# Attention scores as 32-row products of two units side by side, with scores and transposes in one bank

## The reference

```
x = x + 0.5 * ffn(layernorm(x))
x = x + attn(layernorm(x))
x = x + 0.5 * ffn(layernorm(x))
```

## Time and profile before

| | us |
|---|---|
| median of 3 runs (lowest, highest) | 1555.97 (1555.27, 1557.31) |
| span of the profiled execution | 1558.5 |
| PE busy | 1341.3 (86%) |
| DVE busy | 924.5 (59%) |
| ACT busy | 645.8 (41%) |
| POOL busy | 246.7 (16%) |
| starts of the first and of the last scores product | 526.59 and 1166.33 |

### The profile page before, as it was taken

How to read it: one execution, slowest core, us unless ns; L and a number is a source line. 1 busy time by engine, 2 the same in 40 slices (tenths; PEclk the granted TensorE clock), 3 DMA queues, 4 the chain that set the end, 5 groups by cost and what they waited for, 6 DMA issues and landing times.

```text
span 1558.5 us, 32504 instructions
## 1 busy us (share of the span) xinstructions
PE 1341.3 (86%) x8323; PEld 858.5 (55%) x8324; DVE 924.5 (59%) x3760; ACT 645.8 (41%) x2323; POOL 246.7 (16%) x279
## 2 busy tenths in 40 slices
PE   4412799999996899989899999989994699999996
PEld 4411466666664456656566565656653366666664
DVE  5789444444443567787687877787784244444442
ACT  1114322232222476656566665656661132222221
POOL 4323001000102101021111112020212101100100
PEclk9999999999998899999999999999996799999998
DMA  9500442000002101020201111020206221000000
GB/s 301 206 28 31 171 151 58 13 13 13 17 13 88 48 21 42 22 56 21 57 9 38 33 32 46 21 56 21 56 9 242 59 58 55 17 13 13 13 17 14
DMA packets 57278, 85.55 MB, mean 55 GB/s; under 512 B 8848, under 2 KB 40848, under 8 KB 57168
## 3 DMA queue, kind: packets, MB, share of 16 engines
q1 hardware_dynamic: 50352, 65.49, 13.7%
q0 software_dynamic: 6816, 18.81, 3.4%
HBM read 45.81 MB, written 27.97 MB: 47 GB/s over the span
## 4 chain that ended last, share of the span: by engine, by line
PE 66%; DVE 12%; issue 6%; ACT 2%; POOL 2%; DMA 1%; SPq 1%; another core or an unknown queue 1%; DVEq 0%; ACTq 0%; POOLq 0%
PE bank L797 24%; PE bank L926 9%; PE bank L749 9%; PE bank L815 9%; PE bank L952 6%; PE bank L886 4%; DVE w_all L1364 3%; DVE w_all L1373 2%; PE bank L912 2%; DVE hb L1210 2%; PE bank L963 2%; ACT sl L629 2%; PE bank L763 1%; PE bank L899 1%; POOL sorted_rows L504 1%
## 5 line engine op out<-in xcount | busy, mean ns | idle before, releaser
L709 ACT ACTIVATE w_all<-w_all 128x128 f32<-128x128 f32 x896 | 349.7, 393 | 223.1 <-DVE w_all L1364 222.0
L797 PE MATMUL bank<-w_all,xt 128*128 x1680 | 391.2, 383 | 11.5 <-DVE xt L1222 3.5
L1364 DVE CUSTOM_DVE_ANT_0 w_all<-bank,w_all 128x128 f32<-128x128 f32 x896 | 207.3, 287 | 133.8 <-PE bank L926 123.5
L797 PEld LDWEIGHTS bank<-w_all,xt 128*128 128x128 f16 x1680 | 165.3, 98 | 196.7 <-issue 37.3
L1210 DVE SCALAR_TENSOR_TENSOR hb<-bank,ew,sl 128x512 f32<-128x512 f32 x140 | 105.1, 751 | 207.2 <-ACT sl L629 207.2
L815 PE MATMUL bank<-w_all,ht 128*128 x1680 | 206.2, 273 | 1.2 <-DVE yt L1235 1.2
L629 ACT ACTIVATE sl<-bank,back 128x512 f32<-128x512 f32 x140 | 95.9, 685 | 238.6 <-PE bank L797 221.8
L749 PEld LDWEIGHTS bank<-ident,w_all 128*128 128x128 f32 x896 | 112.6, 142 | 119.9 <-issue 113.2
L815 PEld LDWEIGHTS bank<-w_all,ht 128*128 128x128 f16 x1680 | 164.2, 98 | 19.4 <-issue 1.7
L709 ACT ACTIVATION_READ_ACCUMULATOR w_all<-w_all 128x1 f32 x896 | 169.8, 189 | 0.0
L1373 DVE COPY w_all<-bank 128x512 f32<-128x512 f32 x224 | 153.7, 686 | 1.3 <-PE bank L749 1.2
(11 more groups left out here) (163 smaller groups left out, 1585.5 us busy)
## 6 DMA issues: line engine op xcount, KB each, us to landing
big<-sorted_rows SPq DMA_DIRECT2D x70, 130.5 KB
saved<-w_all SPq DMA_DIRECT2D x16, 512.0 KB
w_all<-saved SPq DMA_DIRECT2D x4, 2048.0 KB, 14.2
w_all<-mid SPq DMA_DIRECT2D x9, 512.0 KB, 3.6
big<-in_L_attn_hidden_states SPq DMA_DIRECT2D x8, 512.0 KB, 4.2
w_all<-in_L_ffn_gate_w SPq DMA_DIRECT2D x8, 512.0 KB
w_all<-in_L_ffn_up_w SPq DMA_DIRECT2D x8, 512.0 KB
w_all<-in_L_ffn_down_w SPq DMA_DIRECT2D x8, 512.0 KB
```

Source lines behind the costliest of these rows:

```text
L709: a = nc.scalar.activation(prob[:, u % NB, h], sbias[:, u % NB, h], ACT.Exp, bias=nmax[:, u % NB, h:h + 1], scale=-1.0, accum_out=rsum[:, ...
L797: mm = nc.tensor.matmul(bank[2 * e + w][:], xt[:, hx, c, :], flat(gu16[:, bass.ds(g * E + e, 1), w, hw, c, :]), start=(i == 0), stop=(i == ...
L1364: i = nc.vector.tensor_tensor_reduce(out=sbias[:, u % NB, h], in0=bank[u % 2][:, h * W:(h + 1) * W], in1=nbias[:, (u % NQ) * HQ + h], scal ...
```

## The change

1. `scores` handles two units of a window at once, every second step. Each of its four products has only 32 rows as its contraction (2 heads), the 32 rows of quarter q, and 256 columns: two key images (one for each head of the pair), so the zeros are needed only between two neighbouring heads. The order is: chunk 0 of unit q0, chunk 0 of unit q0 + 1, chunk 1 of q0, chunk 1 of q0 + 1. The two units lie in different 32-row groups of the array and go to different banks.
2. A unit has one bank, u % 4, for its scores and then for its transposes. So the scores of units u + 2 and u + 3, issued at even u, wait for `copy_pt(u - 1)`; `turn` has no wait for a bank.
3. The heads of a unit change: quarter q has heads 2q, 2q + 1, 8 + 2q, 9 + 2q. Its four value products go to four different strips of 32 partitions; odd quarters accumulate on even ones. The columns of `Wv` and `bv` (by eight small POOL copies) and the rows of `Wo` (by eight DMAs in place of one) are permuted to fit.
4. `km` is now written by ACT: each key block is copied twice, scaled by a mask of zeros and ones, with a masked bias (two small DVE operations and four that make the mask, once). `kt`, the 16 DMAs per batch, their waits and the two memsets of `km` go. There are two `km`, one for even and one for odd batches.
5. The loads of `Wo` and `bo` move behind the loads of the first two batches of activations. POOL waits for them ahead of its first `accumulate`, PE ahead of the first output projection.

```diff
-        km = big[:, 0:H * S].rearrange("p (h s) -> p h s", h=H)
+        km = [big[:, k * 2 * DC * S:(k + 1) * 2 * DC * S].rearrange("p (c e s) -> p c e s", c=DC, e=2) for k in range(2)]
...
+        def head_at(q, i):
+            return (i // 2) * HC + 2 * q + i % 2
+        def slot_at(q, i):
+            return (q // 2) * HC + 2 * i + q % 2
...
-            sp.dma_start(wo_s, Wo.rearrange("(c p) n -> p c n", p=P)).then_inc(aw_loaded, 16)
-            sp.dma_start(bo_s, bo.partition_broadcast(P)).then_inc(aw_loaded, 16)
+            def load_wo():
+                wo_rows = Wo.rearrange("(c m l e i) n -> c e l i m n", c=2, m=DC, l=2, e=2)
+                for k in range(HC):
+                    sp.dma_start(wo_s[k * HD:(k + 1) * HD], wo_rows[k // 4, (k // 2) % 2, k % 2]).then_inc(wo_loaded, 16)
+                sp.dma_start(bo_s, bo.partition_broadcast(P)).then_inc(wo_loaded, 16)
...
                 if not last:
-                    sp.wait_ge(k_ready, b * DC + 2 * DC)
-                    sp.wait_ge(s_done, b * UNITS + 4 * NQ + OPEN)
-                    mask_keys(b + 1, 0)
                     sp.wait_ge(xa_ready, (prep_use(b + 1) + 1) * TB)
                     load_batch(b + 2)
                     shift_values(b + 1, 1 - par)
-                    sp.wait_ge(s_done, b * UNITS + UNITS + OPEN)
-                    mask_keys(b + 1, 1)
...
             load_batch(1)
+            load_wo()
...
+            for m in range(DC):
+                for c in range(2):
+                    pool.tensor_copy(wv_to[:, :, m, c], wv_from[:, :, c, m]).then_inc(wv_ready, 1)
+                    pool.tensor_copy(bv_to[:, m, c], bv_from[:, c, m]).then_inc(wv_ready, 1)
+            pool.wait_ge(wo_loaded, 16 * WO_LOADS)
...
-            def copy_k(b, m):
+            def copy_k(b, par, m):
                 act.wait_ge(proj_done, b * NPROJ + (m + 1))
-                if m == 0:
-                    act.wait_ge(km_loaded[1], b * (16 * HC) + OPEN)
-                nc.scalar.activation(kt[:, m, :], bank[6 + m][:], ACT.Identity, bias=qkb[:, 1, m:m + 1]).then_inc(k_ready, 1)
+                for e in range(2):
+                    a = nc.scalar.activation(km[par][:, m, e, :], bank[6 + m][:], ACT.Identity, bias=kb[:, e, m:m + 1],
+                                             scale=kmask[:, e:e + 1])
+                a.then_inc(k_ready, 1)
...
-            def scores(b, par, u, early):
-                n, q = divmod(u, NQ)
+            def scores(b, par, u, freed):
+                n, q0 = divmod(u, NQ)
                 if u == 0:
-                    pe.wait_ge(km_loaded[0], (b + 1) * (16 * HC) + OPEN)
+                    pe.wait_ge(k_ready, (b + 1) * DC)
                     pe.wait_ge(q_ready, (b + 1) * DC)
-                if u == 3 * NQ:
-                    pe.wait_ge(km_loaded[1], (b + 1) * (16 * HC) + OPEN)
-                if not early:
-                    pe.wait_ge(sb_ready, b * UNITS + (u - 1))
-                nc.tensor.matmul(bank[u % 2][:].rearrange("p (h k) -> p h k", h=HQ),
-                                 qt[par][:, q * HQ // HC, n * STRIDE:n * STRIDE + W],
-                                 km[:, q * HQ:(q + 1) * HQ, n * STRIDE:n * STRIDE + W],
-                                 start=True, stop=True).then_inc(s_done, 1)
-            def turn(b, u, early):
+                if freed is not None:
+                    pe.wait_ge(pt_ready, freed)
+                win = slice(n * STRIDE, n * STRIDE + W)
+                for c in range(DC):
+                    for q in (q0, q0 + 1):
+                        rows = slice(q * HS, (q + 1) * HS)
+                        mm = nc.tensor.matmul(bank[q][:, c * 2 * W:(c + 1) * 2 * W].rearrange("p (e k) -> p e k", e=2),
+                                              qt[par][rows, c, win], km[par][rows, c, :, win], start=True, stop=True)
+                        if c == DC - 1:
+                            mm.then_inc(s_done, 1)
+            def turn(b, u):
                 pe.wait_ge(p_ready, b * UNITS + (u + 1))
-                if not early:
-                    pe.wait_ge(pt_ready, b * UNITS + (u - 1))
                 for h in range(HQ):
-                    tr = transpose(bank[2 + u % 2][:, h * W:(h + 1) * W], prob[:, u % NB, h])
+                    tr = transpose(bank[u % NQ][:, h * W:(h + 1) * W], prob[:, u % NB, h])
...
-                    m, pair = divmod((q * HQ + h) // 2, HC // 2)
-                    mm = nc.tensor.matmul(bank[4 + (par + n) % 2][HS * pair:HS * (pair + 1), m * W:(m + 1) * W],
-                                          va[par][:, n, q * HQ + h, :], pt_s[:, u % 2, h * W:(h + 1) * W],
-                                          start=(h % 2 == 0), stop=(h % 2 == 1))
+                    m = q // 2
+                    mm = nc.tensor.matmul(bank[4 + (par + n) % 2][HS * h:HS * (h + 1), m * W:(m + 1) * W],
+                                          va[par][:, n, slot_at(q, h), :], pt_s[:, u % 2, h * W:(h + 1) * W],
+                                          start=(q % 2 == 0), stop=(q % 2 == 1))
...
-                    if ahead(b, u, last):
+                    if u % 2 == 0 and ahead(b, u, last):
                         b2, u2 = ahead(b, u, last)
-                        scores(b2, par if u2 > u else 1 - par, u2, False)
-                    turn(b, u, first_ and u < 2)
+                        scores(b2, par if u2 > u else 1 - par, u2, None if first_ and u == 0 else b * UNITS + u)
+                    turn(b, u)
...
-                nc.vector.tensor_copy(pt_s[:, u % 2], bank[2 + u % 2][:]).then_inc(pt_ready, 1)
+                nc.vector.tensor_copy(pt_s[:, u % 2], bank[u % NQ][:]).then_inc(pt_ready, 1)
```

More of the change, by code:

```diff
@@ L58 @@
 NPROJ = 2 * DC + TB
-ATTN_LOADS = 9
+ATTN_LOADS = 7
+WO_LOADS = 9
+APADS = 2
+VPERM = 8
+MASK_STEPS = 4
 SHIFTS = 2
@@ L181, in macaron_kernel @@
         xb = part(TB, D)
-        kt = part(DC, S)
         sbias = part(NB, HQ, W)
@@ L196, in macaron_kernel @@
         qkb = part(3, DC)
+        kmask = part(2)
+        kb = part(2, DC)
+        kbits = part(1)
         inv_count = part(NWIN)
@@ L200, in macaron_kernel @@
         assert NGU * CH >= at[0] and at[0] - DC * D - D >= NGU * CH * (G - 1) // G
+        wv_in = sbias[:, 0].rearrange("p h k -> p (h k)")
+        bv_in = sbias[:, 1, 0:2].rearrange("p h k -> p (h k)")
         ct = sb("ct", [P, 2, DC, W])
@@ L331, in _ @@
         def _(sp):
-            for s in km_loaded:
-                sp.sem_inc(s, OPEN)
             def load_x(r, par):
@@ L410, in load_batch @@
                 sp.dma_start(xb, rows_of(b)).then_inc(xb_loaded, 16)
[L412 to L418, removed]
             def shift_values(b, par):
@@ L551, in _ @@
                 for half in range(2):
-                    pool.wait_ge(*((icount_made, 2 * n + half) if n or half else (apads_made, 3)))
+                    pool.wait_ge(*((icount_made, 2 * n + half) if n or half else (apads_made, APADS)))
                     pool.memset(inv_count[half * STRIDE:(half + 1) * STRIDE, n:n + 1],
@@ L557, in _ @@
             pool.wait_ge(aw_loaded, 16 * ATTN_LOADS)
+            wv_from = wv_in.rearrange("p (d c m l e i) -> p d c m e l i", d=DC, c=2, m=DC, l=2, e=2)
+            wv_to = wv_s.rearrange("p d (m c e l i) -> p d m c e l i", m=DC, c=2, e=2, l=2)
+            bv_from = bv_in.rearrange("p (c m l e i) -> p c m e l i", c=2, m=DC, l=2, e=2)
+            bv_to = bv_s.rearrange("p (m c e l i) -> p m c e l i", m=DC, c=2, e=2, l=2)
+            for m in range(DC):
[3 more added lines that the diff above has]
+            pool.wait_ge(wo_loaded, 16 * WO_LOADS)
             def accumulate(b, par, n):
@@ L731, in _ @@
             copy_xnt(prep_use(0))
-            copy_k(0, 0)
-            copy_k(0, 1)
+            copy_k(0, 0, 0)
+            copy_k(0, 0, 1)
             copy_q(0, 0, 0)
@@ L880, in _ @@
             pe.wait_ge(aw_loaded, 16 * ATTN_LOADS)
[L881 removed]
+            pe.wait_ge(apads_made, APADS)
             def project(m, w):
@@ L890, in project_v @@
             def project_v(b, t, ranked):
+                pe.wait_ge(wv_ready, VPERM)
                 if t in (0, 2):
@@ L1005, in batch @@
                             t = int(s[1])
+                            if t == 0:
+                                pe.wait_ge(wo_loaded, 16 * WO_LOADS)
                             project_out(b - 1, 1 - par, t, (v_ready, b * TB + TB) if t < 2 else None)
@@ L1031, in _ @@
             pe.wait_ge(v_ready, TB)
-            scores(0, 0, 0, True)
-            scores(0, 0, 1, True)
+            scores(0, 0, 0, None)
             two_by_two(pe, batch)
@@ L1337, in _ @@
             dve.wait_ge(y_ready, NS + OPEN)
-            nc.vector.memset(km[:, 0:H // 2], 0.0).then_inc(km_zero, 1)
+            mask = Chain(mask_step, 0)
+            mask(nc.vector.tensor_single_scalar(kbits.bitcast(I32), token_no[:, 0:1], 4, ALU.arith_shift_right))
+            mask(nc.vector.tensor_single_scalar(kbits.bitcast(I32), kbits.bitcast(I32), 1, ALU.bitwise_and))
```

(9 more changed lines are left out.)

19 lines of the change are left out of this document (8 added, 11 removed).

## The result

The kernel after takes 1601.72 us (median of 4 runs, 1592.89 to 1611.11) against 1555.62 (1550.70 to 1557.31) for the one before: ratio 1.03, 95% interval 1.0256 to 1.0344. It is slower, as forecast, but by 46 us where +9 was expected. The profiled execution took 1599.55 us, and its span, from the first to the last instruction, is 1596.6. The 1558.5 given for the kernel before is a span too, so it is compared here with 1596.6.

A forecast was written before the change was run, and what follows sets the result against it. PE bound the attention stage; after the change a PE-DVE loop through the shared bank would. Six batches +6, batch 0 +2, batch 7 +2, start -1 made +9: 1567 to 1568 us profiled, 1565 us median, range 1538 to 1630.

The forecast's parts named there:

- the loop: Attention stage: PE and DVE wait on each other through the shared bank; a clean pair costs 4.37 us, 4.12 before.
- rival A: Scores on PE: the 32-row products don't overlap, so scores take 1.72 us a pair; 1633 us, chance 0.24.
- The 2.5 taken off: End of the sum: the profiled execution, 1567 to 1568 us, is 2.5 above the median, giving 1565 us.
- Scores of a pair: PE in attention: a load of 0.10 us and 0.97 of columns, between 0.86 and 1.08, against 1.72 of columns before.
- Values: PE in attention: a unit's value products stay at 0.57 us.
- rival B: Value products on PE: all four go at once, `values` falling from 0.57 to about 0.25 us; 1540 us, chance 0.18.
- Rival C: DVE in attention: its lag already cost time before, so the loop costs nothing net; 1550 to 1556 us, chance 0.08.
- +1.0: Batch 1: pairs of steps sum to 81.04 us against 80.06, a loss applied to each of six batches, +6.
- Start: Start of the kernel: `Wo` and `bo` leave the front of the first activations, two issues of 0.51 us; -1.0 us.
- Key copies: ACT copies each key block twice, +2 x 0.69 us a batch, costing nothing; 1.4 a batch if its cover went.
- The eight copies on POOL: Start: they end before the v projections, some 10 us after POOL is free; otherwise each late microsecond counts once.

The follow-up runs named there:

- fill3: The kernel after, with the four value products of each even quarter issued four times; 1577.22 us, ratio 1.0129 to the kernel before.
- unpaired: The kernel after with its 32-row products, but scores one unit at a time, each waiting for `copy_pt` two units back; 1655.25 us, ratio 1.0641 to before.
- turn_twice: The kernel after, with each of the four transposes of a unit issued twice; 1590.23 us, ratio 1.0229 to the kernel before.
- four_strips: The kernel before, 128-row scores one unit at a time, with heads regrouped so a unit's four value products lie in four strips; 1537.49 us, ratio 0.9877.
- paired_128: The kernel after, with scores contracting over all 128 rows, which isn't attention; 1600.45 us, ratio 1.03 to the kernel before.
- own_banks: The kernel after, with scores in banks 0 and 1 and transposes in 2 and 3; 1536.32 us, ratio 0.984 to the kernel before.

## Why the prediction was right in sign and wrong in size

- **The step that failed** is the one that prices every row at full clock. The prediction had no term for the clock, since before holds 1.00 in the batches of the earlier trace rows. Batch 1 loses about 8.4 of its 88.18 us to half clock (1.43 + 4.67 + 2.09 + 0.19). Over batches 1 to 6 the loss is of the same size: their mean is 88.2, while the medians of those pairs that ran at full clock sum to 79.6 (2-3 and 26-27 from `fill3`). That sum is a little low, as in batches 2 and 4 steps 26-27 are long at full clock too (8.19 in batch 4 of after, over 9 in before). About 8 in each of six batches is 48, as much as the 46 us by which after is slower, and batches 0 and 7, at 0.89 and 0.81, lose more. By these rows after would be no slower than before at full clock, 1540 to 1550 us; that is an estimate, and no run of after held the clock.
- **What was luck.** The forecast's "slower" stood on the loop, by which the eight batches were to cost 10 us more. The loop came as priced, but the values were cheaper, and by the estimate above the terms of the sum come to no loss. Slower came true through the clock, which the sum lacked. That 1602 lies within 1538 to 1630 is luck as well: the upper end was set by rival A, which didn't come. The 2.5 taken off at the end of the sum is the distance of a span from a median of execution times; it does no harm, as 1565 is that median plus 9.
- **What lowers the clock.** It is at 0.84 to 0.85 with 32-row scores, whether PE idles 13% (after) or 1% (`unpaired`), and at 0.98 to 0.99 when only the rows are made 128. More 128-row work (`turn_twice`, `fill3`) brings it back. That the 32-row scores lower the clock is shown. It isn't a matter of how many of the numbers are zeros: in `four_strips` the keys of a head are zero outside 16 of its 128 rows, in after outside 16 of 32, and the clock is 1.00 there and 0.84 here. What it is in the rows at work that the clock answers to is not shown. The Trainium skill, TensorE: Matmul & The Clock Gate, What's actually happening, ties the clock to how busy PE has been. By that `unpaired`, busy for 99%, would have held full clock, and `paired_128` would have had the clock of after, which is as busy; the rows above show neither.
- **Scores of a pair.** 0.10 + 0.97 was forecast, 1.06 measured. Rival A (nothing overlaps) did not come.
- **The loop.** 4.37 forecast, 4.40 measured, and its way through the shared bank shown by `own_banks`. At full clock these pairs came as worked out: 8-9 took 5.27 (5.26), 14-15 5.04 (5.03), 16-17 4.96 (4.94), 22-23 5.97 (5.87). Others didn't: 24-25 took 6.03 (6.64).
- **Values.** Kept at 0.57, measured 0.36. This term was mis-sized, and it is rival B's mechanism, at two thirds of its size (B said 0.25): products on four strips take less than on two. It pays where B said, 12-13 took 6.63 (7.02) and 18-19 7.14 (7.53). B's 1540 lies near the estimate above; it lacked the clock as well.
- **Rival C** holds in part. Before's batches 1 to 6 have a mean of 83.3, not the 80.06 of batch 1: PE waits 13.0 us in the middle ahead of values for `copy_pt`. Carrying +1.0 over from batch 1 to all six was too simple. How much of such waits the longer steps of after hide wasn't measured.
- **Start.** -1.0 forecast, -2.9 measured: the first activations' load is issued at 497.54, not 500.50; 1.9 of the 3.0 the queue was ahead before it came to the two issues left out (497.54 against the 499.48 at which before issues `Wo`), 1.2 of it from the first weight load on. Why it was ahead wasn't tried. Key copies cost nothing that shows, as forecast: PE has no wait for ACT's copies in the middle. The eight copies on POOL end at 511, ahead of the v projections at 518.6.

## What to carry to other kernels

When a change makes products use fewer rows of the array, look at the granted clock of the stage before and after, not at busy time alone: here 32-row scores take 1.06 of PE a pair and not 1.92, and PE ran at half clock for a third of the stage. When a wait moves to a buffer's later release, follow both queues round once; if the path comes back to its start with no slack, its length is the new step time where nothing else is longer, and buffers of their own for the two uses open it. On such a stage more computation can be faster: full-row scores, or products repeated in PE's idle time.

## What the runs showed of the hardware that was not expected

- PE at 99% busy with its clock at 0.85 (`unpaired`). At half clock its work takes nearly twice as long: 1.12 becomes 2.07 for four scores records.
- Small float32 products overlap by how many different row groups or strips they use, in either order tried: eight value records in 0.63 on two strips, 0.43 on four; eight 32-row scores records in 1.13 or 1.14, against 2.00 on 128 rows.
- One unit at a time, scores on 32 rows make a pair of steps 0.59 longer than on 128 rows, even at full clock (4.64 against 4.05). Nothing here shows why.
- Repeating transposes raises the clock (0.84 to 0.97, `turn_twice`) as repeating value products does (0.84 to 0.96, `fill3`).
